# One-hots times factors: sixteen per-partition-scalar steps a quad in place of a comparison and a product

## The reference, cut to what matters

```python
xs = x[:, :C] @ W_s ; xv = einsum('nci,cf->nfi', x[:, C:], W_v)   # node table, gathered at idx_j
u = r_ij / norm(r_ij) ; Yv = Y1 * u                               # 3 numbers an edge
h = softplus(f_ij @ Wf1 + bf1) - log(2)                           # 128 hidden numbers an edge
W = (h @ Wf2 + bf2) * rcut_ij[:, None]
x_ij = concat([s2 * W[..], v2 * W[..], ...])                      # messages
agg = segment_sum(x_ij, idx_i, num_segments=n)                    # sum over the edges of a node
```

## Time and profile before

| what | value |
|---|---|
| three runs | 1504.84, 1506.69, 1510.11 us; median 1506.69 |
| span of the profiled execution, first to last instruction | 1503.6 us (no other time of this execution is listed) |
| busy, whole span | PE 91%, DVE 66%, POOL 50%, ACT 42% |
| busy in 26 to 440 us | PE 332.4, DVE 268.8, ACT 210.6, POOL 315.6 of 414.0 us |
| granted PE clock, mean of the span | 0.946 |

### The profile page before, as it was taken

One profiled execution on the slowest core, in us unless ns is written; L12 is line 12 of the kernel. 1 busy time (PEld: TensorE's weight loads), 2 busy tenths in 40 slices (PEclk: granted clock), 3 DMA queues, 4 the chain that ended last, 5 costly groups with the idle time before them and its releaser, 6 DMA issues.

```text
span 1503.6 us, 24451 instructions
## 1 busy us (share of the span) xinstructions
PE 1368.8 (91%) x6707; PEld 646.0 (43%) x6708; DVE 987.4 (66%) x2481; ACT 626.5 (42%) x1097; POOL 752.3 (50%) x772
## 2 busy tenths in 40 slices
PE   6577998868879999999999999974999999999997
PEld 4254444435534444444444444462433343433333
DVE  7946666567737777777777777765655565546554
ACT  5455555545425666666666666571101111111110
POOL 4777777777766555566556555604312211211121
PEclk9667999999789999999999999996999999999999
DMA  5665333333249888888888888582342551524513
GB/s 201 225 222 162 114 117 116 116 110 107 103 139 295 249 248 246 250 250 249 250 246 253 249 248 246 152 334 66 71 161 63 191 186 28 195 70 143 193 28 94
DMA packets 125874, 262.50 MB, mean 175 GB/s; under 512 B 21073, under 2 KB 64808, under 8 KB 125147
## 3 DMA queue, kind: packets, MB, share of 16 engines
q0 software_dynamic: 48416, 141.37, 31.4%
q1 hardware_dynamic: 77410, 120.57, 24.0%
HBM read 204.35 MB, written 63.66 MB: 178 GB/s over the span
## 4 chain that ended last, share of the span: by engine, by line
PE 62%; POOL 21%; issue 8%; DVE 4%; DMA 3%; ACT 1%; POOLq 0%; SPq 0%; DVEq 0%; ACTq 0%
PE psum L1376 20%; POOL edge_list L456 19%; PE psum L1868 17%; PE psum L1880 8%; PE psum L1389 7%; PE psum L1384 5%; PE psum L1371 2%; POOL slot_list L1800 1%; DMA edge_list<-rec,place 1%; DMA out_x<-out_sums 1%; PE psum L1875 1%; DMA slot_list<-pair,slots 1%; PE psum L1571 0%; PE psum L1486 0%; PE psum L637 0%
## 5 line engine op out<-in xcount | busy, mean ns | idle before, releaser
L1263 POOL DMA_INDIRECT shared<-node_table,shared x328 | 310.0, 945 | 212.5 <-DVE msg L1344 128.8
L456 POOL DMA_INDIRECT edge_list<-rec,place x313 | 315.4, 1008 | 96.7 <-issue 94.8
L1346 DVE TENSOR_TENSOR msg<-shared,psum 128x768 f32<-128x768 f32 x328 | 310.2, 946 | 0.0
L1376 PE MATMUL psum<-wf,hT 128*128 128x512 f32 x656 | 305.6, 608 | 2.7 <-ACT psum L1301 2.1
L1868 PE MATMUL psum<-shared,zT 128*64 128x512 f32 (+1 forms) x960 | 295.8, 597 | 1.6 <-DVE zT L1986 1.6
L1301 ACT COPY psum<-bias 128x512 f32<-128x512 f32 x328 | 193.3, 590 | 211.7 <-DVE msg L1346 194.2
L1344 DVE TENSOR_TENSOR msg<-shared,psum 128x256 f32<-128x256 f32 x328 | 135.8, 414 | 135.1 <-PE psum L1376 121.1
L1868 PEld LDWEIGHTS psum<-shared,zT 128*64 128x64 f32 (+1 forms) x960 | 114.6, 159 | 180.6 <-issue 178.6
L1376 PEld LDWEIGHTS psum<-wf,hT 128*128 128x128 f32 x656 | 118.1, 190 | 154.5 <-issue 138.0
L1828 POOL DMA_DIRECT2D ids<-slot_list x20 | 11.5, 577 | 291.3 <-DVE zN L1955 266.8
L1880 PE MATMUL psum<-shared,hidT 128*64 128x512 f32 (+1 forms) x480 | 152.7, 596 | 2.3 <-DVE hidT L2007 2.3
(11 more groups left out here) (355 smaller groups left out, 1527.1 us busy)
## 6 DMA issues: line engine op xcount, KB each, us to landing
shared<-edge_list SPq DMA_DIRECT2D x332, 130.0 KB
shared<-in_L_ffn_w_gate SPq DMA_DIRECT2D x8, 2048.0 KB, 9.1
shared<-in_L_ffn_w_up SPq DMA_DIRECT2D x8, 2048.0 KB, 14.8
shared<-in_L_ffn_w_down SPq DMA_DIRECT2D x8, 2048.0 KB, 19.5
shared<-node_table,shared POOLq DMA_INDIRECT x328
edge_list<-rec,place POOLq DMA_INDIRECT x313
raw<-in_records SPq DMA_DIRECT2D x19, 256.0 KB, 3.7
xrow<-in_x SPq DMA_DIRECT2D x10, 250.0 KB
```

The lines of the kernel that those rows point to most:

```text
L456: nc.gpsimd.indirect_dma_start(out=edge_list, out_offset=bass.IndirectOffsetOnAxis(ap=place[:n_, c:c + 1].bitcast(U32), axis=0), in_=rec[: ...
L1263: nc.gpsimd.indirect_dma_start(out=gat[:, k % G, :], out_offset=None, in_=table, in_offset=bass.IndirectOffsetOnAxis(ap=ix, axis=0)).then_ ...
L1346: nc.vector.tensor_tensor(m[:, 1:7, :].rearrange("p (a i) f -> p a i f", a=2), g[:, P:D].rearrange("p (i f) -> p i f", i=3).unsqueeze(1).t ...
L1376: nc.tensor.matmul(WP[k % TS][:], hT[:, (k // TS) % 2, (k % TS) * P:(k % TS + 1) * P], wf2[:], start=False, stop=True, skip_group_check=Tr ...
```

## The change

`eq` and its semaphore go. `record_known` writes the four blocks of each column with four `tensor_scalar` instructions: iota compared with `at_f` of the column (one number a partition), the result times one factor of the column (one number a partition), straight into the record. They are 16 instructions a quad, 32 numbers a partition each; the last one raises `hot_done`. The waits for the record buffer, for `cc` and the copy of node numbers stay. All else is as it was.

```diff
-            eq = sbi("eq", [P, 2, QC, W])
...
-                    def equal(u):
-                        iota = const[:, C_IOTA:C_IOTA + W].unsqueeze(1)
-                        n_ = min(QC, EK - u * QC)
-                        if u >= 2:
-                            dve.wait_ge(hot_done, u - 1)
-                        nc.vector.tensor_tensor(eq[:, u % 2, 0:n_], iota.to_broadcast([P, n_, W]),
-                                                at_f[:, u * QC:u * QC + n_].unsqueeze(2).to_broadcast([P, n_, W]), ALU.is_equal).then_inc(eq_done, 1)
-
                     def record_known(u):
                         n_ = min(QC, EK - u * QC)
                         if u >= 3:
                             dve.wait_ge(placed[u % 3], 16 * QC * (u // 3))
                         r = rec[:, u % 3, 0:n_]
                         nc.vector.tensor_copy(r[:, :, RDST].bitcast(I32), from_i[:, u * QC:u * QC + n_])
-                        dve.wait_ge(eq_done, u + 1)
                         if u % FG == 0:
                             dve.wait_ge(cc_done, u // FG + 1)
-                        nc.vector.tensor_tensor(r[:, :, RO:RDST].rearrange("p j (v w) -> p j v w", v=4),
-                                                eq[:, u % 2, 0:n_].unsqueeze(2).to_broadcast([P, n_, 4, W]),
-                                                cc[:, u // FG % 2, u % FG * QC:u % FG * QC + n_, :].unsqueeze(3).to_broadcast([P, n_, 4, W]), ALU.mult).then_inc(hot_done, 1)
+                        for j in range(n_):
+                            c = u * QC + j
+                            for v in range(4):
+                                ins = nc.vector.tensor_scalar(r[:, j, RO + v * W:RO + (v + 1) * W], const[:, C_IOTA:C_IOTA + W], at_f[:, c:c + 1],
+                                                              cc[:, u // FG % 2, u % FG * QC + j, v:v + 1], ALU.is_equal, ALU.mult)
+                        ins.then_inc(hot_done, 1)
...
-                    equal(0)
...
-                            equal(u)
+                            pass
```

More of the change, by code:

```diff
@@ L291, in gps_layer @@
             ranked = sem("buckets_ranked")
-            quad_mm, eq_done, quad_ln, x_read, hot_done = (sem(n_) for n_ in (
-                "radial_mm", "equal_done", "radial_ln", "records_made", "onehots_done"))
+            quad_mm, quad_ln, x_read, hot_done = (sem(n_) for n_ in (
+                "radial_mm", "radial_ln", "records_made", "onehots_done"))
             placed = [sem(f"records_placed{i}") for i in range(3)]
```

## The result

The changed kernel takes 1583.5 us (median of four runs, 1580.1 to 1586.3) against 1506.3 before (four runs by now): 1.051 times the time, 95% interval 1.049 to 1.053. Forecast were 1592 and a range of 1545 to 1640.

The account below looks back on a forecast made before the run. POOL's scatters set the front's pace; DVE would become the bound. 2.7 + 209.4 - 90.4 - 32.4 = +89.3 us, tail -4.1, front about +85; 1503.6 + 85.2 = 1588.8, plus 3.1 gives 1592 us, range 1545 to 1640.

Parts of the forecast that it names:

- The bound changed hands: Front: DVE becomes the bound at about 6.3 us a quad against POOL's 5.3; front end near 525 us.
- the stage sums: Front's five stages: DVE's busy time plus 2.72 us a quad overflows each stage, e.g. 58.5 us where it had 45.3.
- The price of a step: DVE's 16 new steps a quad: 0.22 us each, 3.52, less 0.80 removed, gives 2.72 us more a quad.
- The quarter of the contention: DVE steps meeting scatters: a quarter of the 40 ns excess seen at L1133, added to 0.211, giving 0.22 us.
- The waits: DVE's idle time in the front: all 90.4 us at L882 go, and 32.4 of 40.4 us of other waits.
- PE's clock: Front: PE's clock could fall as PE gets idler; third stage at 0.91 some 107 us, under DVE's 120: nothing.
- The tail: End of the front, after the last full record: lagging POOL has 6.3 us left instead of 10.4, giving back 4.1.
- Hidden steps: Rival, 4%: steps on DVE cost about 0.09 us, load stays under POOL's pace; 1500 us.
- Steps at 0.155: Rival, 10%: each DVE step costs 0.155 us, +1.68 a quad fills the slack unevenly, over by 22 us; 1529 us.
- DVE and POOL in each other's way: Rival, 14%: steps take turns with scatter generation, POOL needs 560 us instead of 412 and stays the bound; 1655 us.

Follow-up runs that it names:

- e2: Changed kernel with both per-partition scalars of the 16 steps replaced by constants; 1506.5 us, ratio 0.999 to the kernel before.
- e10: Changed kernel with one two-scalar step a column over 128 elements, every block taking the first factor; 1497.0 us, ratio 0.994 to the kernel before.
- e1: Changed kernel with only the comparison in each of the 16 steps, multiplication and second scalar left out; 1530.7 us, ratio 1.016 to the kernel before.
- e5: No one-hots at all: neither comparison and product of the kernel before nor the steps, those record parts zeroed once; 1522.9 us, one expert block more.
- e6: Kernel before with its product of 512 elements split into four of 128, one a column; 1506.1 us against 1508.6, ratio 0.9983.
- e4: Changed kernel with 12 of the 16 steps a quad, one-hots for one of four factors left out; 1533.5 us, ratio 1.017 to the kernel before.
- e11: Changed kernel with the factor replaced by the constant 2 (two operations, one per-partition scalar); 1571 us in its only run, with 46 SiLUs against 42.

## Why the prediction was right, point by point

**The bound changed hands, as forecast.** The step that carried the result was the comparison of 2.72 us more a quad with the idle time of each stage. From record to record (start of the copy at L882, now L873) the stretches from quad 1 to 9, 23, 43, 57 and 77 grew by 12.1, 11.8, 12.7, 8.7 and 27.3 us. Forecast were, from the stage sums, 13.2, 6.1, 19.7, 7.4 and 26.8. DVE's waits for record buffers were gone but for two (at quads 16 and 19), POOL waited 1.3 us a quad for records (about 1 forecast), and the front ended at 515 (525 forecast). The second stretch is the one that was too low: DVE's slack there lies behind quad 13, and the quads ahead of it overflow by themselves, so the mean over the stretch hid it. The third was too high, mostly by the price of a step (20 x 0.27 = 5.4 us). The prediction has a second sum in these stages that it did not use: they add up to 73.2 us, where its own sum has 209.4 - 90.4 - 32.4 = 86.6 for the same quads, since the stages leave DVE no idle time at all. Measured are 72.6. That the stage sums come so near is luck: with the price as measured they would be 73.2 - 77 x 0.27 = 52.4, and the other 20 us are idle time that DVE still had.

**The price of a step: 0.209, not 0.22 us.** The value worked out from L1133 (0.211) was right. The quarter of the contention that I laid on top was hardly there: the steps of full quads average 0.209, with the lowest quad at 0.206. Sixteen steps are 3.35 us. By the two busy times (455.8 - 267.4 in the like stretch of before) DVE has 188.4 us more work over 77 quads, net 2.45 us a quad, where I had 209.4. So 0.90 us a quad went, not 0.80. Part of that is the comparison, which takes 0.25 us in the mean and not 0.20, since it counts with its whole 0.28 us where a wait follows it; the product takes 0.61 as read. The price of a quad is the term that was mis-sized most.

**The waits.** Idle time of DVE in that stretch went from 136.3 to 23.7 us, 112.6 less; I had 122.8 (90.4 + 32.4). Still there are 7.8 us at the record buffer, where I had taken all of them away, and 10.8 for others, where I had 8. So errors of 21 and 10 us worked against each other, and that the forecast is off by 9 us only is in part luck: 2.4 + 188.4 - 112.6 = +78.2 at the last full record, measured as 506.06 - 427.84, for a forecast of +89.3.

**PE's clock** was let go at no cost. The granted clock is 0.85 in the stretch against 0.87, with PE busy 341.0 of 479.5 us. Whether that cost nothing is not shown: the chain that ended last passes through PE too (L592, L470 and L572 with 2%, 1% and 1% of the span). No run holds the clock fixed.

**The tail** gave back 2.9 us (from record to edge load 12.1, now 9.2) for a forecast 4.1. Behind the front the span grew by 3.5 us more; I had nothing there. The spread of the runs is 6 us, and I can't tell it from that.

**Rivals.** *Hidden steps*: not so for these, but e2 shows the very case, at 0.087 us: no time lost, and none won that can be told (1506.5 us, scatters at 996 ns). The Trainium skill, "VectorE: DVE Perf Modes", section on the TRN2 errata, has 58 cycles plus elements over the mode's factor, an estimate of 77 ns. Measured are 87 ns with no per-partition scalar, which comes close, and 148 and 209 ns with one and two. The same page, section on the perf-mode tiers, gives such an instruction on fp32 in SBUF twice the base rate, 0.52 ns an element by the page's clock, and e10's 0.49 agrees. *Steps at 0.155*: e1, with 0.148, took 1531 us, where I had 1529. *DVE and POOL in each other's way*: refuted as a cost. The scatters grew shorter with the steps, 979 from 1008 ns, while DVE ran steps more than half of the time. The Trainium skill, "SBUF — State Buffer", section "SBUF: two separate sides", has GpSimd and a VectorE instruction in a two-port mode shut each other out for whole instructions. By the trace a step's longest duration is 547 ns for a median of 294 and the mean only 17 above it, so no step waits for a scatter's 0.96 us. The two do meet, at one point: 177 of the 1252 steps took over 350 ns, and 166 of these end within 0.06 us of the end of a scatter. They are some 115 ns longer than the median, and from start to start the quads are still 0.209 us a step.

**What holds the scatters up** in the kernel before was left open in the prediction. Counted over the timelines, of eleven scatters beside L959 (two SBUF tensors, 512 elements) eight lasted over 1.03 us; in the changed kernel eight of ten beside the same line (now 952), and of 221 beside steps fourteen, eight of which also met line 952. But of 94 beside the product (L886), which reads two SBUF tensors of 512 elements as well, only twenty-nine did, and without comparison and product (e5) twenty-five of 313 are still that long, against fifty-four before. Removing the comparison and product (e5) gives 984 ns, splitting one of them (e6) 993. This agrees with a scatter that at times waits for the end of a VectorE instruction with two SBUF tensors; it isn't proved: no run held all else fixed, and what decides which scatters wait stays open.

## What to carry to other kernels

Before an instruction is cut into many short ones, find the start-to-start distance of the short form with its very operands; in these steps each per-partition scalar cost 60 ns, and 96 elements more only 47. Compare the growth with the idle time of that engine stage by stage, in the part of the program that it runs in, for the first of it is free and the rest is paid in full. Where an experiment leaves out data on which the program's course depends, read it at a point ahead of that dependence.

## What the runs showed of the hardware that I had not expected

- A second operation in a VectorE step costs nothing (232 against 234 ns), while each per-partition scalar costs 60 ns, be it that of the comparison or that of the product (173, 234, 294 ns median duration with none, one, two; 32 elements).
- A VectorE step and a scatter that POOL generates get in each other's way almost only at the scatter's end: 166 of the 177 steps over 350 ns end within 0.06 us of it.
- Steps that read one SBUF tensor at some two elements a time (0.49 ns an element by e10, where comparison and product differ by 1.06), back to back, did not lengthen the scatters that POOL was generating (979 ns mean, the shortest of all kernels here but e4 and e11 with 977 and 976, which have such steps too).
